# Graph network kernel: GpSimd clears its 512 spare columns behind every other block of gathers, and once a step in the last graph pass

## The reference, cut to what matters

```
h = x @ W
msg = h[src] * norm[:, None]
agg = jax.ops.segment_sum(msg, dst, num_segments=n)
agg = agg + h * (dis * dis)[:, None]
...
# last network, six such layers, widths 128-64-32-16-32-64-128
h = h @ W; msg = h[row] * norm[:, None]
agg = jax.ops.segment_sum(msg, col, num_segments=num_nodes)
return agg + b
```

## Time and profile before

| | |
|---|---|
| median of 3 runs | 10529.21 us (10516.9 to 10536.39) |
| the profiled execution, own time | 10513.06 us |
| its span in the profile | 10510.6 us |
| VectorE busy | 8002.5 us (76%) |
| GpSimd busy | 7840.4 us (75%) |
| TensorE matmul busy | 6426.3 us (61%) |
| ScalarE busy | 5904.7 us (56%) |
| mean granted TensorE clock | 0.702 of full speed |

### The profile page before, as it was taken

The page is one execution under the profiler, slowest core; times in us unless marked ns, Lnnn a source line. Parts: engine busy times, 40 slices in busy tenths (PEclk is TensorE's granted clock), DMA queues, the critical chain, the costliest instruction groups (busy, mean ns, idle before and its releaser), DMA issues. The chain is left out here.

```text
span 10510.6 us, 142293 instructions
## 1 busy us (share of the span) xinstructions
PE 6426.3 (61%) x32436; PEld 5258.3 (50%) x32436; DVE 8002.5 (76%) x33105; ACT 5904.7 (56%) x13869; POOL 7840.4 (75%) x7586
## 2 busy tenths in 40 slices
PE   6037666667774666667755666786457675654444
PEld 3026655555664666667755666674235443432222
DVE  8359899956667999999988888655558777874444
ACT  0026577767776999978957777432125443432222
POOL 7767688867776888766637777687777777878887
PEclk8569988878886555578868888665558765765555
DMA  3999888832223777634424555464336443432222
GB/s 114 330 299 314 286 289 289 289 123 75 76 74 121 234 236 235 207 126 139 142 87 160 173 175 177 145 172 120 92 104 183 143 116 99 139 111 65 63 65 60
DMA packets 1019500, 1694.47 MB, mean 161 GB/s; under 512 B 304877, under 2 KB 535080, under 8 KB 1018594
## 3 DMA queue, kind: packets, MB, share of 16 engines
q1 hardware_dynamic: 782752, 1361.06, 38.8%
q0 software_dynamic: 175936, 218.82, 9.3%
q10 hardware_dynamic: 59970, 105.49, 2.9%
HBM read 988.03 MB, written 707.78 MB: 161 GB/s over the span
## 5 line engine op out<-in xcount | busy, mean ns | idle before, releaser
L1351 POOL DMA_INDIRECT g_got<-scaled,row_src x2352 | 2230.1, 948 | 751.5 <-issue 631.8
L903 DVE SCALAR_TENSOR_TENSOR g_sums<-g_got,first,g_sums 128x128 f32<-128x128 f32 (+3 forms) x3136 | 871.6, 278 | 1159.5 <-DMA g_got<-scaled,row_src 1148.4
L299 PE MATMUL g_a_p_z<-sb_L_gnn_W,g_a_u_t 128*128 128x128 f32 (+3 forms) x2574 | 603.8, 373 | 592.5 <-DVE g_sums L1073 197.4
L1186 ACT COPY g_a_u_t<-g_a_p_t 128x512 f32<-128x512 f32 (+3 forms) x495 | 224.8, 454 | 1222.2 <-PE g_a_p_t L1138 637.3
L907 DVE SCALAR_TENSOR_TENSOR g_sums<-g_sums,cont,g_got 128x128 f32<-128x128 f32 (+3 forms) x3128 | 881.3, 282 | 0.0
L299 PEld LDWEIGHTS g_a_p_z<-sb_L_gnn_W,g_a_u_t 128*128 128x128 f32 (+1 forms) x2574 | 443.1, 245 | 759.9 <-ACT g_a_u_t L1186 398.3
L299 PE MATMUL g_bb_p_z<-sb_L_gnn_W,g_bb_u_t 128*128 128x128 f32 (+2 forms) x4302 | 755.8, 336 | 84.7 <-DVE g_bb_z L1078 77.0
L299 PEld LDWEIGHTS g_bb_p_z<-sb_L_gnn_W,g_bb_u_t 128*128 128x128 f32 x4302 | 676.0, 237 | 135.6 <-issue 108.9
L1186 ACT COPY g_bb_u_t<-g_bb_p_t 128x1024 f32<-128x1024 f32 (+2 forms) x294 | 233.6, 795 | 774.6 <-PE g_bb_p_t L290 774.1
L2475 POOL DMA_INDIRECT gb_got<-x,row_src x392 | 404.8, 1033 | 242.1 <-POOLq L178 138.1
L458 POOL DMA_INDIRECT f_got<-in_x,idx_dst x396 | 463.2, 1170 | 139.8 <-issue 120.1
(11 more groups left out here) (496 smaller groups left out, 23955.6 us busy)
## 6 DMA issues: line engine op xcount, KB each, us to landing
raw<-gb_u SPq DMA_DIRECT2D x98, 768.0 KB, 3.9
xs<-f_o ACTq DMA_DIRECT2D x97, 516.0 KB
f_x<-in_x ACTq DMA_DIRECT2D x97, 512.0 KB
g_bb_own<-in_x SPq DMA_DIRECT2D x97, 512.0 KB
wide<-g_bb_o SPq DMA_DIRECT2D x97, 512.0 KB
g_bb_own<-wide SPq DMA_DIRECT2D x97, 512.0 KB
g_bb_res<-in_x SPq DMA_DIRECT2D x97, 512.0 KB
x<-g_bb_o SPq DMA_DIRECT2D x97, 512.0 KB
```

What stands on the lines that cost most here:

```text
L299: last = nc.tensor.matmul(dst_psum[0:p, q * g * width:(q * g + n) * width], turned_tile[0:n * k, q * P:q * P + p], weight[0:n * k, 0:n * w ...
L903: nc.vector.scalar_tensor_tensor(out=self.firsts, in0=new, scalar=first[:, col], in1=self.firsts, op0=ALU.mult, op1=ALU.add).then_inc(run_ ...
L1186: last = nc.scalar.copy(to, source)
L1351: pool.indirect_dma_start(got[b.s4][:, c * row:(c + 1) * row], None, table, bass.IndirectOffsetOnAxis(ap=index[:, b.n * CH + c:b.n * CH + ...
```

## The change

In every pass but g8, `rest` returns without doing anything for even blocks, so that the memset follows every other block of four gathers, and eight gathers stand in a row between two of them. In g8 the stage `(rest, 0, NBE)` is taken out: the memset follows the scatters alone, from step 4 on.

```diff
                         def rest(b):

+                            if not scatters and b.n % 2 == 0:
+                                return
                             if rests.k:
                                 pool.wait_ge(pool_step, rests.k)
                             nc.gpsimd.memset(idle[:, :], 0.0).then_inc(pool_step, 1)
...
                         if scatters:
-                            pipeline(pool, [(gather, 0, NBE), (rest, 0, NBE), (na.scatter, 4, NBA), (rest, 4, NBA)])
+                            pipeline(pool, [(gather, 0, NBE), (na.scatter, 4, NBA), (rest, 4, NBA)])
                             na.scatters_done()
```

## The result

The changed kernel takes 10391.27 us (median of 4, 10388.18 to 10393.8) against 10525.06 for the kernel before (median of 4 runs, one more than the 3 ahead of the prediction): 133.8 us less, ratio 0.9872 with a 95% interval of 0.9855 to 0.9889. The forecast was 10401, 128 less than the 10529.2 of that time.

What follows compares the result with a forecast made beforehand. GpSimd's stream was taken to bound g3 to g8: g4 and g6 40, g8 40, g3 18, g5 10, g7 19, g1 1 make 128 us off 10529.2, giving 10401. Own range 10383 to 10419; 8 in 10: 10380 to 10560.

Steps and rivals of the forecast that it cites:

- 0.41 us a memset: GpSimd's gather stream: each memset removed gives 0.54 + 0.17 less the 0.30 gap that comes back, 0.41 us.
- The stream sets g3 to g8: GpSimd's gathers, gaps and memsets set the length of passes g3 to g8; VectorE's sums hold g1.
- g3, g4, g6, g7: Graph passes, 49 memsets fewer in each: 18, 20, 20 and 19 us taken; g3 bounds 14 to 20, g7 8 to 20.
- g8: Last pass, gathers and scatters: 98 memsets fewer at 0.41 us, 40 us taken.
- g1: Pass where GpSimd waits for VectorE's sums: at most 5 us gained, 1 taken.
- g5: Pass with thin VectorE cover, 6.6 us: GpSimd would come to wait for VectorE; 10 us taken, bounds 8 to 20.
- Rival 1: Engines behind hold the gathers: g3, g5, g6, g7 give only 8 us each, gain 92, 10437 us; chance 0.08.
- Rival 2: Gathers have a floor: no long stretch below about 1.34 us each, so time stays at 10529; chance 0.10.
- Rival 3: Runs of eight in g3 to g7 bring long gathers as in cg: slower, 10546 to 10642 us; chance 0.20.

Runs made afterwards that it cites:

- the kernel with one input in PSUM: Changed kernel plus two extra VectorE additions of 128x384 a block in g4, second input in PSUM, into an unread spare tile: 10403.51 us, one run.

## Why the prediction was right

- **The time.** The gain was 6 us more than forecast, and the median of before fell by 4 with its fourth run; together they make the 10 us between 10401 and 10391.
- **0.41 us a memset.** 0.406 by the passes (19.9 / 49), and the account behind it (0.54 + 0.17 less the 0.30 that comes back) held at 64 and at 1024 columns: 0.03 and 0.84 (0.97 + 0.17 - 0.30) a memset by the rows.
- **The stream sets g3 to g8.** Shown by the dose for g4: more columns, fewer columns and none at all move it by the sum of the memsets' time and nothing else. g3, g6 and g7 follow in the same way (568.9 to 569.0 with 1024 columns, 491.3 or 491.4 with 64, 488.1 or 488.2 with none), and g8 goes 1172.8, 1089.9, 1018.5, 1013.1. g5 follows it upwards only.
- **g3, g4, g6, g7:** taken 18, 20, 20, 19; measured 18.6, 19.7, 19.9, 19.5. No gather of g3 waited even without any memset (488.2), the least certain of my covers; what TensorE is behind there is paid on the way to g4, 23 to 39 us from profile to profile.
- **g8:** taken 40, measured 37.9 here and 37.8 alone. The steps gave 0.395 each and not 0.41, and near the end, where nothing but scatters is left, these wait longer for ScalarE's rows: 2.6 us in all instead of 0.8. This end I had left out.
- **g1:** taken 1, measured 0.8 in this pair of profiles and nothing when all its memsets went. That is less than g1 differs from one execution to the next, so the 1 is neither borne out nor refuted.
- **g5:** the mechanism was right, its size was off. The step was: "With gathers at 5.20 a block VectorE falls behind 1.6 per eight steps, 16 us over 80 blocks, more than the cover; then GpSimd waits for VectorE." It falls behind about half as fast: block 22's own-row add ended 4.2 us after its last gather, block 86's, at the same place of the rhythm, 10.6; that is 0.8 in eight blocks, so eight steps of VectorE's took about 42.4 and not the whole 43.2. The trace of before had this slack, and I overlooked it. After the 15th block VectorE was not past all waits for gathers: between the adds of blocks 22 and 86 (7916 to 8263) it still had five.

```profile
DVE g_sums L903 <- DMA g_got<-scaled,row_src: 5.2, 5, 3.0
```

That is 0.65 in eight steps, which leaves 42.6 of the 43.2. The cover just held. The add of block 92, the tightest, and the first gather of block 96:

```profile
8252.60 0.23 DVE L1038 TENSOR_TENSOR g_sums<-g_a_own,g_sums 128x64 f32<-128x64 f32 x1
...
8253.42 0.95 POOL L1353 DMA_INDIRECT g_got<-scaled,row_src  x1 [0.17 <-issue]
```

8252.83 against 8253.42: 0.6 us left of the 6.6 of before. No gather waited, so they gave all of their 19.9, and the backlog was paid behind them: 17.3 instead of 11.6 from the last gather to g6. Net 14.2, where I took 10 in bounds of 8 and 20. That this is the edge shows in the kernel with one input in PSUM: with the same g5 it had 12 waits of up to 0.9 for L1038 in its profile, and 511.8 instead of 507.7. So which side of the edge an execution falls on is in part luck.
- **The sum.** That 128 came so near to the 129.8 of the table is partly luck: g5 gave 4 more than taken and g8 2 less.
- **Rival 1** (the engines behind hold the gathers) holds for the gathers of g5 only once the second half of its memsets is gone too. But the length of g5, gathers and way together, is set behind GpSimd from the first half on: 539.2 before, 525.0 with half (507.7 + 17.3), 525.9 without any (508.5 + 17.4).
- **Rival 2** (a floor at 1.30 or above) fell with 392 gathers at 1.248.
- **Rival 3** (long gathers) has its cause shown and its place excluded: it needs a long operation with two SBUF inputs, which g3 to g8 do not have. The range of 1.42 to 1.81 that I gave for the long gathers of cg was too narrow: 175 of its 784 are above 1.03, half of them under 1.42, the longest 1.955. I had given it 0.20 for the lack of a row with a sustained run; what I had in the rows of cg spoke against it already.

The version without any memset beats both kernels: 10275.61, 2.3% under the kernel before beside it, and by the medians 1.1% under the changed one, though these two did not run beside each other. No run here showed anything that a memset does for this kernel.

## What to carry to other kernels

When one engine's stream is back to back with nothing but issue gaps over a whole pass, a thing put into it costs its way from end to start less the gap that was there anyway; count that, and then look for how long the engines behind can follow, by the lag between what they consume and what they hand back, over the whole pass and not over one block. A backlog that does not stop the stream is still paid at the pass's end, so take the gathers and the way to the next pass together. Before a long gather is put down to the run it stands in, look at what VectorE does beside it and where the inputs of that lie.

## What was not expected of the hardware

An indirect gather of 128 rows keeps 1.248 us for 392 in a row, with rows of 64 to 256 bytes and DMA engines busy 38 to 63% of the time (g3, g4, g6 and g7 without memsets). A memset on GpSimd started without the 0.30 gap that a gather has before it, so that 64 columns cost 0.03 us between gathers: 170, 544 and 970 ns for 64, 512 and 1024 columns, 0.83 ns a column and some 117 ns fixed. And an addition that reads PSUM for one of two inputs leaves gathers at 0.94 us, where one that reads only SBUF stretched 56 of 392, the longest to 1.29.
